# Four chained graph layers on one core: GpSimd waits for each group's gathers to land in two edge loops, and TensorE signals once per step in one of them

## The reference, cut to what matters

```python
# L2, per edge e
h = silu(edge_scalars @ W_fc1 / sqrt(10));  w = h @ W_fc2 / sqrt(100)
m00 = w00 * y0[src] * sh0;  m11 = w11 * sum_c(y1[src] * sh1) / sqrt(3)
m01 = w01 * y0[src] * sh1;  m10 = w10 * y1[src] * sh0
sums = segment_sum(concat(m00, m11, m01, m10), dst)
# L3, per edge e
w_ij = mlp(edge_feats, rad) + mlp(chi_scalar, sph)
alpha = (q[dst] * w_ij * k[src]).sum(-1) / sqrt(16) * cutoffs
out = segment_sum(alpha * v[src], dst) / 16
```

## Time and profile before

| what | us |
|---|---|
| median of 3 runs | 9544.22 |
| lowest and highest of them | 9513.62, 9572.33 |
| profiled execution, span | 9589.4 |
| convolution's edge loop, in that span | 3558.8 to 6327 |
| attention's edge loop, in that span | 6430 to 9545 |

### The profile page before, as it was taken

How to read it: one execution, slowest core, us unless ns; L and a number is a source line. 1 busy time by engine, 2 the same in 40 slices (tenths; PEclk the granted TensorE clock), 3 DMA queues, 4 the chain that set the end, 5 groups by cost and what they waited for, 6 DMA issues and landing times. The chain is left out here.

```text
span 9589.4 us, 196015 instructions
## 1 busy us (share of the span) xinstructions
PE 7798.7 (81%) x51013; PEld 5815.8 (61%) x51014; DVE 6070.5 (63%) x12579; ACT 5243.3 (55%) x9302; POOL 3242.1 (34%) x3274
## 2 busy tenths in 40 slices
PE   5999999888699978888888777777777777777775
PEld 3656666677599966566556444445555555555554
DVE  7988998899844455555555455555555555555556
ACT  3666666788577754444444333345555555555553
POOL 0000000000000015555555556644555555454554
PEclk8999999999899988888888777788888888898897
DMA  3333333566466622222222111124555555454554
GB/s 114 138 132 137 139 136 138 190 225 223 149 183 183 183 85 58 57 57 58 56 58 57 43 43 44 44 70 144 149 147 151 152 148 148 143 159 144 149 157 124
DMA packets 627968, 1178.30 MB, mean 123 GB/s; under 512 B 215083, under 2 KB 288220, under 8 KB 608469
## 3 DMA queue, kind: packets, MB, share of 16 engines
q1 hardware_dynamic: 498618, 859.56, 28.2%
q0 software_dynamic: 129280, 317.93, 11.8%
HBM read 900.47 MB, written 276.57 MB: 123 GB/s over the span
## 5 line engine op out<-in xcount | busy, mean ns | idle before, releaser
L2250 POOL DMA_INDIRECT att_kv_rows<-kv_dram,att_stage x1616 | 1607.9, 995 | 1502.8 <-DVE att_msgs L2396 1013.5
L2005 POOL DMA_INDIRECT conv_rows<-y_dram,conv_stage x1616 | 1566.7, 969 | 1198.2 <-DVE conv_msgs L2077 678.1
L851 PE MATMUL att_mlp<-mlp_w,mlp_hid 128*128 128x128 f32 x6272 | 918.9, 296 | 397.8 <-issue 391.8
L851 PEld LDWEIGHTS att_mlp<-mlp_w,mlp_hid 128*128 128x128 f32 x6272 | 824.6, 206 | 471.7 <-issue 464.9
L1974 ACT ACTIVATE conv_hid<-conv_hid_ps 100x512 f32<-100x512 f32 x408 | 243.5, 597 | 1413.1 <-DMA y_dram<-mean_nodes_both 983.8
L695 PE MATMUL conv_part<-conv_msgs,conv_hot 128*128 128x256 f32 x3232 | 931.9, 437 | 50.1 <-issue 49.0
L2014 PE MATMUL conv_hid_ps<-conv_scalars,conv_w 10*100 10x512 f32 x816 | 529.1, 731 | 387.9 <-ACT conv_hid L1974 292.7
L695 PEld LDWEIGHTS conv_part<-conv_msgs,conv_hot 128*128 128x128 f32 x3232 | 690.5, 225 | 162.2 <-issue 64.0
L2223 ACT ACTIVATE acc<-att_q_ps 128x512 f32<-128x512 f32 x404 | 239.3, 592 | 985.9 <-DMA kv_dram<-conv_nodes_qkv 571.8
L842 PE MATMUL att_mlp<-mlp_feats,mlp_w 64*128 64x512 f32 x1568 | 558.4, 769 | 260.1 <-ACT mlp_hid L862 146.6
L235 PE MATMUL count_ps<-count_cols,count_rows 128*128 128x392 bf16 x3920 | 730.1, 331 | 8.6 <-DVE count_cols L201 8.6
(11 more groups left out here) (276 smaller groups left out, 15863.0 us busy)
## 6 DMA issues: line engine op xcount, KB each, us to landing
c_dram<-count_counts SPq DMA_DIRECT2D x392, 392.0 KB, 2.3
mean_counts<-c_dram SPq DMA_DIRECT2D x343, 448.0 KB, 3.4
w_dram<-mlp_w SPq DMA_DIRECT2D x404, 256.0 KB
att_w_rows<-w_dram SPq DMA_DIRECT2D x404, 256.0 KB
soft_counts<-c_dram SPq DMA_DIRECT2D x98, 1024.0 KB, 4.9
mlp_feats<-in_feats SPq DMA_DIRECT2D x405, 192.0 KB
soft_counts<-c_dram SPq DMA_DIRECT2D x49, 1088.0 KB, 5.0
att_lanes<-lo_dram SPq DMA_DIRECT2D x404, 128.0 KB
```

The lines of the kernel that those rows point to most:

```text
L851: ins = nc.tensor.matmul(self.w_ps[:, t * D:(t + 1) * D], self.hid[:, n, t * P:(t + 1) * P], self.w1[:, n, :], start=n == 0, stop=n == 2 * ...
L2005: pool.indirect_dma_start(rows[:, s, t, :], None, y_dram, bass.IndirectOffsetOnAxis(ap=stage[:, s, t:t + 1], axis=0)).then_inc(gathered[s] ...
L2250: pool.indirect_dma_start(kv_rows[:, s, t, :], None, kv_dram, bass.IndirectOffsetOnAxis(ap=stage[:, s, t:t + 1], axis=0)).then_inc(gathere ...
```

## The change

Both loops: after a group's four gathers GpSimd waits until all of them have landed, before it turns to the next group.

Convolution: a step of TensorE is now `second`, `first`, a quarter of a unit (`tensor_quarter`), `lane_sums`, in this order, and only `lane_sums` signals (`c.sums_done`). ScalarE's silus of `hid` and of the unit (`scalar_quarter`), DVE's `message` (from the third group on), DVE's take of a unit (`vector_of`) and SP's loads wait for that one semaphore instead of `w_done`, `hid_sum` and `w_sum`. DVE's wait for the weights of g+2 thus lies behind `first`, the quarter and the sums of step g. `tensor_skip` adds the counts that the attention expects. The attention's other engines are as before.

```diff
+    def tensor_quarter(self, nc, pe, u, s):
+        if s < 2:
+            if s == 0:
+                pe.wait_ge(self.feats_in, 16 * (u + 1))
+            pe.wait_ge(self.hid_done, 2 * self.NC * u + 2 * s + 2)
+            for n in range(2):
...
+        else:
+            if s == 2:
+                pe.wait_ge(self.hid_done, 2 + 2 * self.NC * (u + 1))
+                pe.wait_ge(self.w_taken, u + 1)
...
@@ SP, convolution
                         if s % 2 == 1:
-                            sp.wait_ge(hid_sum, S * i + s + 1)
+                            if first:
+                                sp.wait_ge(hid_sum, s + 1)
+                            else:
+                                sp.wait_ge(c.sums_done, S * i + s + 1)
                             load_scalars(s // 2, S * (i + 1) + s - 1)
                     if unit:
-                        mlp.sync_body(sp, U_CONV + i, 1, first)
+                        if not first:
+                            mlp.store(sp, U_CONV + i - 1)
+                        sp.wait_ge(c.sums_done, S + S * i + 2)
+                        mlp.load(sp, U_CONV + i + 1)
@@ ScalarE, convolution
-                        act.wait_ge(w_done, S * i + s + 1)
-                        silu(S * (i + 1) + s, s)
+                        act.wait_ge(c.sums_done, S + S * i + s + 1)
+                        silu(s)
+                        if unit and s < 2:
+                            mlp.scalar_quarter(nc, act, s)
                         if s < 2 or not last:
                             lane_hot(nc, act, c, (s + 2) % S, S * i + s + 2)
-                        if unit:
-                            mlp.scalar_step(nc, act, U_CONV + i, s, 1)
@@ GpSimd, convolution; the same line in the attention
+                        pool.wait_ge(gathered[s], 16 * T * (i + 1))
@@ TensorE, convolution
-                        pe.wait_ge(hid_done, g + 4)
-                        first(s, i + 2)
                         pe.wait_ge(msg_done, 1 + g + 1)
                         second(g + 2, (s + 2) % S)
+                        pe.wait_ge(hid_done, g + 4)
+                        first(s, i + 2)
+                        if unit:
+                            mlp.tensor_quarter(nc, pe, U_CONV + i, s)
                         lane_sums(nc, pe, c, s, g, 2 * i + s // 2, msgs[:, s])
...
-                        if unit:
-                            mlp.tensor_step(nc, pe, U_CONV + i, s, 1)
@@ VectorE, convolution
-                    dve.wait_ge(w_done, g + 1)
+                    if first and s < 2:
+                        dve.wait_ge(w_done, 1)
+                    else:
+                        dve.wait_ge(c.sums_done, S + g - 1)
...
                         if unit and s == 1 and not first:
-                            mlp.vector(nc, dve, U_CONV + i - 1)
+                            dve.wait_ge(c.sums_done, S + S * i)
+                            mlp.vector_of(nc, dve, U_CONV + i - 1)
```

More of the change, by code:

```diff
@@ L869, in vector, with scalar_quarter, vector_of, tensor_skip @@
                                 self.b1[:, 0].unsqueeze(1).to_broadcast([P, T, D]), ALU.add).then_inc(self.w_taken, 1)
+    def tensor_quarter(self, nc, pe, u, s):
[4 more added lines that the diff above has]
+            for n in range(2):
+                half = slice(n * P // 2, (n + 1) * P // 2)
+                nc.tensor.matmul(self.hid_ps[:, n], self.w0[half, s * P:(s + 1) * P], self.feats[half, :], start=True, stop=True)
+        else:
+            if s == 2:
+                pe.wait_ge(self.hid_done, 2 + 2 * self.NC * (u + 1))
+                pe.wait_ge(self.w_taken, u + 1)
+            for t in range(T // 2 * (s - 2), T // 2 * (s - 1)):
+                for n in range(2 * self.NC):
+                    nc.tensor.matmul(self.w_ps[:, t * D:(t + 1) * D], self.hid[:, n, t * P:(t + 1) * P], self.w1[:, n, :],
+                                     start=n == 0, stop=n == 2 * self.NC - 1)
+    def scalar_quarter(self, nc, act, s):
+        for n in range(2):
+            nc.scalar.activation(self.hid[:, 2 * s + n], self.hid_ps[:, n], ACT.Silu, bias=self.b0[:, 2 * s + n:2 * s + n + 1]).then_inc(self.hid_done, 1)
+    def vector_of(self, nc, dve, u):
+        dve.wait_ge(self.w_stored, 16 * (u + 1))
+        nc.vector.tensor_tensor(self.w[:], self.w_ps.rearrange("p (t f) -> p t f", t=T),
+                                self.b1[:, 0].unsqueeze(1).to_broadcast([P, T, D]), ALU.add).then_inc(self.w_taken, 1)
+    def tensor_skip(self, pe, units):
+        pe.sem_inc(self.hid_sum, 2 * self.NC * units)
+        pe.sem_inc(self.w_sum, units)
     def tensor_step(self, nc, pe, u, s, per):
@@ L1971, in _, with silu @@
             def _(act):
-                def silu(g, s):
-                    act.wait_ge(hid_sum, g + 1)
+                def silu(s):
                     nc.scalar.activation(hid[:, s], hid_ps[0:100], ACT.Silu, scale=10 ** -0.5).then_inc(hid_done, 1)
@@ L1977, in body @@
                     for s in range(S):
-                        act.wait_ge(w_done, S * i + s + 1)
-                        silu(S * (i + 1) + s, s)
+                        act.wait_ge(c.sums_done, S + S * i + s + 1)
+                        silu(s)
+                        if unit and s < 2:
+                            mlp.scalar_quarter(nc, act, s)
                         if s < 2 or not last:
                             lane_hot(nc, act, c, (s + 2) % S, S * i + s + 2)
-                        if unit:
-                            mlp.scalar_step(nc, act, U_CONV + i, s, 1)
                 for g in range(S):
-                    silu(g, g)
+                    act.wait_ge(hid_sum, g + 1)
+                    silu(g)
                 for g in range(2):
@@ L2013, in first @@
                     n = s % 2
-                    nc.tensor.matmul(hid_ps[0:100], w1[rows_of(n)], scalars[rows_of(n), s // 2, :], start=True, stop=True).then_inc(hid_sum, 1)
+                    return nc.tensor.matmul(hid_ps[0:100], w1[rows_of(n)], scalars[rows_of(n), s // 2, :], start=True, stop=True)
                 def second(g, s):
@@ L2025, in _ @@
                         pe.wait_ge(hid_done, s)
-                    first(s, 1)
+                    first(s, 1).then_inc(hid_sum, 1)
                 second(0, 0)
-                second(1, 1)
+                second(1, 1).then_inc(w_done, 1)
                 def turns(i, s):
@@ L2051, in _ @@
                     body(i, False, True)
+                mlp.tensor_skip(pe, N_CONV)
                 with pe.Fori(N_CONV, NI) as i:
@@ L2057, in _, with message @@
             def _(dve):
-                def message(i, s):
+                def message(i, s, first):
                     g = S * i + s
@@ L2091, in body @@
                     for s in range(S):
-                        message(i, s)
+                        message(i, s, first)
                         if s == 1 and not first:
```

10 lines of the change are left out of this document (6 added, 4 removed).

## The result

The changed kernel takes 9966.85 us (median of 4 runs, 9964.17 to 9968.19) and the kernel before 9537.56 us in the same job (median of 4): the ratio is 1.0446, interval 1.0418 to 1.0474. It is slower, as forecast, but by 4.5% instead of 1.5%, and 17 us above the range. The profiled execution spans 9963.8 us, 374.4 us more than before's 9589.4.

What follows compares the result with a forecast made beforehand. It took a chain of waits to bound both loops, PE's signals being kept back during gathers and POOL then idling. Floor +73, rest +73 and one signal 0 on 9544 gave 9690 us, own range 9600 to 9830, overall 9440 to 9950.

Steps and rivals of the forecast that it cites:

- The new wait as a floor for POOL: Both loops: issue, landing and restart per group cost POOL 14.70 us a pair against 14.52 before, +73 us.
- the landing: End of last gather to DVE's start, from each loop's first group: 1.66 us convolution, 1.80 us attention, taken as upper ends.
- The sum: Floor +73, rest +73, one signal 0: +146 us, added to the median of 9544 us, giving 9690 us.
- By stage: The floor's change per group against the kernel before: +0.40 us in the convolution, -0.22 us in the attention.
- The rest: Both loops: POOL's waits for DVE beyond the new idle time, at most 584 us; an eighth taken, 73 us.
- The kept-back signals: Both loops: PE's signals to ACT and DVE are held while gathers are issued and under way; pauses let them out.
- Let go when the last one has landed: Kept-back PE signals are released once the last gather has landed; read from waiters starting together 6.4 us after PE's end.
- One signal per step, counted at nothing: Convolution: DVE's 4.7 us later wait and ACT's 5.64 us chain stay hidden under POOL's 7.23 us; 0 us.
- rival C: Convolution: one-signal chain through ACT at half clock takes 10.2 us in a third of unit groups; 9925 us, chance 0.15.
- A: Rival, both loops: pauses end the keeping-back, gathers run at their best, POOL never waits for DVE; 9342 us, chance 0.13.
- B: Rival of no difference, both loops: the floor alone with shorter landings, 14.36 us a pair; 9480 us, chance 0.28.
- the signs listed: Pauses 2.3 to 2.7 us, runs of at most four gathers, loops near 2920 and 3020 to 3080 us, "remote" waits a third.

Runs made afterwards that it cites:

- e10: The changed kernel without GpSimd's two waits, the convolution's one signal per step kept: 9622.93 us, 1.0073 of the kernel before in the same job.
- e11: The kernel before with GpSimd's two waits added, its signals as before: 9958.24 us, 1.0422 of the kernel before in the same job.
- e12: The changed kernel with GpSimd's wait behind every second group only: 9476.21 us, 0.9899 of the kernel before in the same job.
- e13: The kernel before with GpSimd's wait added behind every second group only, in both loops: 9298.58 us, 0.9719 of the kernel before.
- e2: The kernel before with GpSimd's two waits added, signals as before: 10005.23 us, 1.2387 of the kernel before, which took 8076.86 us there.
- e8: The kernel before with GpSimd's two waits added, run again: 10008 us, 1.2393 of the kernel before, which took 8073.03 us there.

## Why the prediction was right and wrong

**The new wait as a floor for POOL: right as a mechanism, its size wrong.** Predicted 7.23 + 7.47 = 14.70 us a pair, measured 15.46. The floor is 0.94 us above before's 14.52 instead of 0.18: 403 x 0.94 = 379 us, the 374 of the spans. This is the step that failed, and within it the landing, which was taken from the first group of each loop. In the convolution the pause came to 2.52 us instead of 2.45, the excess being the turn of the iteration. In the attention it came to 3.15 us instead of 2.59. Of the 0.76 us a pair that the floor was short, 0.56 is the attention's pause, 0.07 the convolution's, and the rest the steps within the groups. POOL's timeline in the changed kernel's attention, first the first group, then four in the steady loop and a load that SP issues among them:

```profile
6656.05 0.94 POOL L2298 DMA_INDIRECT att_kv_rows<-kv_dram,att_stage  x1 [2.63 <-DMA att_kv_rows<-kv_dram,att_stage]
...
8003.50 0.95 POOL L2298 DMA_INDIRECT att_kv_rows<-kv_dram,att_stage  x1 [2.67 <-DMA att_kv_rows<-kv_dram,att_stage]
...
8011.66 0.95 POOL L2298 DMA_INDIRECT att_kv_rows<-kv_dram,att_stage  x1 [2.95 <-issue]
...
8020.09 1.11 POOL L2298 DMA_INDIRECT att_kv_rows<-kv_dram,att_stage  x1 [3.73 <-DMA att_kv_rows<-kv_dram,att_stage]
...
8025.89 0.33 SPq L2230 DMA_DIRECT2D att_w_rows<-w_dram  x1
...
8029.30 0.94 POOL L2298 DMA_INDIRECT att_kv_rows<-kv_dram,att_stage  x1 [4.36 <-DMA att_kv_rows<-kv_dram,att_stage]
```

The first group's pause, 2.63 us, is what was forecast. Later ones vary from that to 4.36 us here (4.51 at the most). What DMA moved in the four later pauses (the last two numbers of a row are the DMA engines' share and GB/s):

```profile
8000.83:8003.50 2.67, 2.41 (x24) 1.64 (x20) 2.45 (x6) 1.79 (x5) 0.00 (x1) 1.00 0.18 52
8008.71:8011.66 2.95, 0.00 (x0) 0.00 (x0) 0.55 (x1) 0.60 (x1) 0.00 (x1) 0.79 0.16 45
8016.35:8020.09 3.74, 3.31 (x10) 1.81 (x11) 3.43 (x7) 1.21 (x2) 0.01 (x2) 0.50 0.37 117
8024.96:8029.30 4.34, 4.25 (x38) 3.31 (x38) 1.55 (x3) 3.52 (x8) 0.00 (x0) 1.00 0.60 190
```

The same holds over the whole loop. The means of its pauses, by the group that follows, with the trace's records of single DMA packets (SP's KB are those moved between the start of the last gather and its last packet, a packet that overlaps in part counted by its share):

| pause before group | pause, us | end of issue to last packet | last packet to next gather | SP's KB meanwhile |
|---|---|---|---|---|
| s = 0 (turn of the iteration) | 2.98 | 1.46 | 1.53 | 3 |
| s = 1 | 3.40 | 2.20 | 1.20 | 281 |
| s = 2 | 3.55 | 2.33 | 1.22 | 404 |
| s = 3 | 2.66 | 1.48 | 1.18 | 15 |

Where SP moves next to nothing, the pause is that of the first group, or 0.3 us more at the turn, whose restart is longer; where its loads and stores are under way, the landing is 0.7 to 0.9 us longer. In the convolution SP moves little, and its last packet comes 1.24 us after the issue in all four places. This is a comparison inside one run; no run takes SP's transfers away. I had called the first group's landing an upper end, since DVE's wake was inside it; it was no bound to what else was on the queues.

**The sum was added to the wrong base.** A floor of POOL's own does not depend on what before takes. The periods of before came from an execution of 9589.4 us, so the difference belonged on that: 9589.4 + 379 = 9968 us, against 9966.85 measured. The prediction added it to the median of 9544 us, and 9544 + 379 = 9923 would still have lain inside the range. The landing and the missing rest together made 9923 of the 9690; these 45 us took it over the upper bound.

**By stage.** +0.40 us a group in the convolution became +0.55, and -0.22 in the attention became +0.39. The sign in the attention hung on the landing: with the forecast pause of 2.59 us it would have stayed under before's 7.69.

**"The rest", an eighth of 584 us: an error of 73 us the other way.** POOL's waits for DVE are 37 us. With the floor as measured the older wait ends under the pause in all but 14 places. The two errors together are 403 x 0.76 = +306 and about -73, which is the way from +146 to +379.

**The kept-back signals: right in the main, and of no use.** The reading of the earlier trace rows held: signals of PE are kept back while gathers follow each other, and a pause lets them out (e10, e11). But POOL's pace with the pauses, 15.46 us a pair, is above that of before with all its kept-back signals (14.52).

The rows shown for it were not the ones that the waiters wait for. By the program's order DVE's L2072 waits there for the weights of one step earlier, and ACT's silu for the `first` ahead of the row shown:

```profile
5706.98 1.16 PE L2019 MATMUL conv_w_ps<-conv_w,conv_hid 100*128 100x128 f32 x8
5709.79 1.10 PE L2014 MATMUL conv_hid_ps<-conv_scalars,conv_w 10*100 10x512 f32 x2
```

These end at 5708.14 and 5710.89, so the two waiters start 10.3 and 7.6 us after them, not 6.4, and two signals that were given almost 3 us apart arrive together. "Let go when the last one has landed" fits the convolution of before: those of its waits with a senseless releaser that end in a pause of POOL do so 1.0 to 2.3 us after the end of issue (the middle 80%), at the median 0.6 us after the gathers' last packet. In the attention two thirds of them end with packets still under way, so there the landing is not shown to be the condition.

**One signal per step, counted at nothing: right under these waits.** e11 (9958 us) against the changed kernel (9957 and 9967 us, other jobs) shows no difference. It is not nothing once POOL leaves room: 0.7% in e10 by the medians. By the profiled executions e10 is 30 us longer than before (9619.2 and 9589.4), and 28 of these are in the convolution's loop; the rest of the 71 us between the medians is that the profiled execution of before was a long one. Between e12 and e13 it is 1.9%. I read this as the chain of rival C, at a smaller price, hidden by POOL in the changed kernel; that the half clock is what makes it is not shown.

**The rivals.** A fell with the landings: its condition on DVE was nearly met (37 us of waits), and there was no gain even so. B was the floor with shorter landings and fell likewise. C's time was the nearest (9925 us), by another mechanism. Of the signs listed, the pause of 2.3 to 2.7 us held for three quarters of the convolution's groups and not in the attention, and neither loop kept the forecast length (2976 us instead of 2920, 3261 instead of 3020 to 3080). No pause under 2 us, no run of over four gathers, POOL's waits for DVE under 300 us and "remote" waits under a third held.

**What stays open**: what decides whether signals are kept back in a job. It is outside the program, as the same kernel does both, and it does not go with the chip's number: jobs of both kinds came from one. It is also open whether the pause must last until the landing: no run has a shorter pause.

## What to carry to other kernels

A wait for a DMA's landing on the engine that issues the next ones costs the landing and the restart each time, here 2.1 to 2.8 us; take the landing from the steady loop with its other transfers and not from its first, quiet turn. A floor is an absolute time: add it up from nothing, or from the very execution whose periods it is compared with. If pauses cure something, ask how few do: every second group gained 2.8%, every group lost 4%, every fourth 1.1%, and where there was nothing to cure every pause was a loss. Where waits have releasers that make no sense, run the kernel before in more than one job: the state that the change aims at may not be there in the next.

## What the runs showed of the hardware that was not expected

- The same kernel before took 8073 and 8077 us in two jobs and 9538 to 9589 us in four, 18% apart, each reproducible inside its job (but for the one run told of above). In the slower ones signals of TensorE reach DVE and ACT up to 10 us late and more while indirect DMAs follow on each other (782 us of ACT's waits in 149 places in e10); in the others no such wait is seen.
- With a pause after every group the time hardly knows the difference: 10005 and 10008 us in the former (e2, e8), 9957 to 9967 in the latter (e11 and the changed kernel).
- The pause for the landing of four gathers of 128 rows of 1024 bytes was 2.63 us in the first group and 3.15 us on the mean over the loop: 2.66 us where SyncE moved 15 KB meanwhile, 3.55 us where it moved some 400 KB.
- After the last packet of the gathers has ended, the next gather starts 1.2 us later, 1.5 to 1.6 us at the turn of an iteration.
